# Six front projections in two rounded passes instead of one fp32 pass, with GpSimd preparing the weights, on one Trainium2 core

## The reference, cut to what matters

```python
def _fp8_linear_pertensor(x, wq, w_scale, in_scale):
    xq = _div_clamp_fp8(x, in_scale)          # divide, clip, round to fp8
    return jnp.einsum('bsi,oi->bso', xq * in_scale, wq) * w_scale
...
ln_out = _ln(hidden_states, ln_w, ln_b)
q = _ln(_fp8_linear_pertensor(ln_out, wq, ...), qln_w, qln_b)
k = _ln(_fp8_linear_pertensor(ln_out, wk, ...), kln_w, kln_b)
v = _fp8_linear_pertensor(ln_out, wv, ...)
core = _gqa(q, k, v)
qx = _ln(_fp8_linear_pertensor(ln_out, wqx, ...), qxln_w, qxln_b)
kx, vx = jnp.split(cond @ w_kv_x.T, 2, axis=-1)
xout = _gqa(qx, _ln(kx, kxln_w, kxln_b), vx)
catq = _div_clamp_fp8(concat([core, xout]), proj_smooth)
x = x + catq @ wproj.T * (proj_in_scale * proj_w_scale)
...
w = lut[idx]          # last block: three 256 x 688 tables of weights
```

## Time and profile before

| | |
|---|---|
| median of 3 runs | 498.17 us (496.26 to 504.01) |
| the profiled execution | 496.25 us, its span 494.5 us |
| mean granted TensorE clock | 0.979 |
| PE busy | 453.7 us (92%), 2305 matmuls |
| DVE busy | 354.5 us (72%) |
| ACT busy | 250.2 us (51%) |

### The profile page before, as it was taken

How to read it: one execution, slowest core, us unless ns; L and a number is a source line. 1 busy time by engine, 2 the same in 40 slices (tenths; PEclk the granted TensorE clock), 3 DMA queues, 4 the chain that set the end, 5 groups by cost and what they waited for, 6 DMA issues and landing times.

```text
span 494.5 us, 6607 instructions
## 1 busy us (share of the span) xinstructions
PE 453.7 (92%) x2305; PEld 308.7 (62%) x2311; DVE 354.5 (72%) x722; ACT 250.2 (51%) x784; POOL 27.3 (6%) x36
## 2 busy tenths in 40 slices
PE   5969898699899999999999999998987999989987
PEld 2424444477768575767667775856743888636566
DVE  5884859749797869699896889886765665435631
ACT  1476788867663786866767577553011330120120
POOL 0000000004000010100010010100020010000000
PEclk9999999769999999999999999999998999999999
DMA  8263210405100374644648753890058477300000
GB/s 309 95 270 137 85 62 25 170 3 192 44 1 1 107 144 120 135 113 100 154 107 212 233 113 101 175 340 1 1 180 340 160 195 179 112 6 1 1 0 21
DMA packets 14046, 58.69 MB, mean 119 GB/s; under 512 B 1792, under 2 KB 2624, under 8 KB 12480
## 3 DMA queue, kind: packets, MB, share of 16 engines
q1 hardware_dynamic: 10992, 41.80, 23.2%
q0 software_dynamic: 3024, 16.52, 16.9%
HBM read 41.53 MB, written 0.26 MB: 85 GB/s over the span
## 4 chain that ended last, share of the span: by engine, by line
PE 71%; DVE 16%; ACT 9%; issue 2%; DMA 1%; SPq 0%; DVEq 0%; ACTq 0%
PE PS L455 10%; PE PS L428 8%; PE PS L430 7%; PE PS L429 7%; PE PS L1035 6%; PE PS L363 5%; PE PS L1514 3%; PE PS L1046 3%; PE PS L475 3%; ACT raw_dt.float L1617 2%; PE PS L502 2%; PE PS L1145 2%; ACT raw_dt.float L1597 2%; ACT zu_dt.float L1628 2%; PE PS L1481 1%
## 5 line engine op out<-in xcount | busy, mean ns | idle before, releaser
L570 ACT ACTIVATE sq_dt.float<-PS 128x128 bf16<-128x128 f32 x256 | 67.3, 278 | 33.6 <-PE PS L430 27.1
L455 PE MATMUL PS<-s_dt.float,ctx_ring_dt.float 128*128 128x512 f32 x128 | 57.7, 593 | 2.0 <-DVE px_dt.float L787 2.0
L428 PE MATMUL PS<-wkc_dt.float32r,ctx_hi_dt.float32r 128*128 128x512 f32 x128 | 54.3, 425 | 0.4
L570 ACT ACTIVATION_READ_ACCUMULATOR sq_dt.float<-PS 128x1 f32 x256 | 53.1, 207 | 0.0
L430 PE MATMUL PS<-wkc_dt.float32r,ctxT_ring_dt.float32r 128*128 128x512 f32 x128 | 50.8, 397 | 0.0
L429 PE MATMUL PS<-wkT_dt.float32r,ctx_hi_dt.float32r 128*128 128x512 f32 x128 | 50.7, 396 | 0.0
L1481 PE MATMUL PS<-wch_dt.float,xs_dt.float 128*128 128x512 f32 x96 | 42.1, 593 | 0.0
L363 PE MATMUL PS<-consts_dt.float 128*128 128x512 bf16 x141 | 34.3, 401 | 6.3 <-DMA consts_dt.float<-in_consts 5.5
L455 PEld LDWEIGHTS PS<-s_dt.float,ctx_ring_dt.float 128*128 128x128 f32 x128 | 23.6, 190 | 25.7 <-issue 23.0
L641 ACT ACTIVATE luttmp_dt.float<-low_bit_dt.float,vec_dt.float,small_dt.float 128x1536 f32<-128x1536 uint8 x24 | 38.4, 1653 | 0.0
L648 DVE SCALAR_TENSOR_TENSOR luttmp_dt.float<-idx_dt.float,luttmp_dt.float 128x1536 f32<-128x1536 uint8 x21 | 36.4, 1750 | 0.0
(11 more groups left out here) (276 smaller groups left out, 844.1 us busy)
## 6 DMA issues: line engine op xcount, KB each, us to landing
lutw_dt.float<-luttmp_dt.float POOLq DMA_DIRECT2D x21, 768.0 KB, 6.7
wch_dt.float<-in_chunks SPq DMA_DIRECT2D x6, 1024.0 KB, 4.8
ctxT_ring_dt.float<-in_ctxT SPq DMA_DIRECT2D x8, 512.0 KB, 3.3
ctx_ring_dt.float<-in_ctx SPq DMA_DIRECT2D x8, 512.0 KB, 3.7
keysT_dt.float<-in_ctxT SPq DMA_DIRECT2D x8, 512.0 KB, 7.4
keys_dt.float<-in_ctx SPq DMA_DIRECT2D x8, 512.0 KB, 9.3
luttmp_dt.float<-in_idx SPq DMA_DIRECT2D x3, 768.0 KB, 6.3
zu_dt.float<-in_wproj SPq DMA_DIRECT2D x1, 2048.0 KB, 7.2
```

What stands on the lines that cost most here:

```text
L428: nc.tensor.matmul(o, x_hi, hi[:, c, :], start=c == 0, stop=False)
L455: last = nc.tensor.matmul(bank(5 + c), keysr[k][:, t, c * 128:c * 128 + 128], sS[k][:, t, :], start=t == 0, stop=t == KT - 1)
L570: last = nc.scalar.activation(sq[:, (4 * hf + g) * D:(4 * hf + g + 1) * D], bank(hf)[:, g * D:(g + 1) * D], ACT.Square, accum_out=ssq[:, k ...
```

## The change

- `xs` stays the fp8 value, rounded into fp32r by the last operation of `round_fp8`; `L1719` is gone. GpSimd multiplies each weight chunk by `in_scale` instead (two instructions of 128 x 1024), copies it rounded into `wch_hi` (128 x 2048), and subtracts that to leave `wch_lo` (128 x 2048). `project(n)` makes four banks from `wch_hi` and then adds the `wch_lo` products: 16 fp32r matmuls for 8 fp32 ones.
- GpSimd waits for the chunk's load, and from chunk 2 on for projection n-2.
- `turn(4)` moves from banks 0 to 3 to the rotating banks 4 to 7, behind the first tile of the step-0 keys; PE's order in the transition is rewritten, and ACT reads projection 5 in two halves around `normalise(4)` and takes its squares earlier.
- DVE's step 0 is `first_step`: score tiles before `quantize_core(1)`, no `term`, `low_bits` at the end. `lut_gap` and `pscale` are computed near the start of the front.
- Table step k moves from loop step k to k+1; `term(6)` and `term(7)` lie in the MoE, ACT's `leaf(6)` in step 7.

```diff
             def project(n):
                 pe.wait_ge(xs_ready, SCALED.index(VARIANT[n]) + 1)
-                pe.wait_ge(ld_chunk[n % 2], 16 * (n // 2 + 1))
+                pe.wait_ge(chunk_hi, n + 1)
                 for q in range(4):
                     j, hf = q // 2, q % 2
                     if n:
                         pe.wait_ge(proj_read, 4 * n - 3 + q)
                     for c in range(CT):
+                        nc.tensor.matmul(bank(q), xs[:, VARIANT[n], c, j * 128:j * 128 + 128],
+                                         wch_hi[n % 2][:, c, hf * 512:hf * 512 + 512], start=c == 0, stop=False)
+                pe.wait_ge(chunk_split, n + 1)
+                for q in range(4):
+                    j, hf = q // 2, q % 2
+                    for c in range(CT):
                         last = nc.tensor.matmul(bank(q), xs[:, VARIANT[n], c, j * 128:j * 128 + 128],
-                                                wch[n % 2][:, c, hf * 512:hf * 512 + 512],
-                                                start=c == 0, stop=c == CT - 1)
+                                                wch_lo[n % 2][:, c, hf * 512:hf * 512 + 512],
+                                                start=False, stop=c == CT - 1)
                     last.then_inc(proj_full, 1)
...
+            def split_chunk(n):
+                pool.wait_ge(ld_chunk[n % 2], 16 * (n // 2 + 1))
+                if n > 1:
+                    pool.wait_ge(proj_full, 4 * (n - 1))
+                for c in range(CT):
+                    scaled_w = nc.gpsimd.tensor_scalar(wch[n % 2][:, c, :], wch[n % 2][:, c, :],
+                                                       col("in_scale", VARIANT[n] * CT + c), None, ALU.mult)
+                step(scaled_w)
+                nc.gpsimd.tensor_copy(wch_hi[n % 2], wch[n % 2]).then_inc(chunk_hi, 1)
+                pool.wait_ge(chunk_hi, n + 1)
+                nc.gpsimd.tensor_tensor(wch_lo[n % 2], wch[n % 2], wch_hi[n % 2], ALU.subtract).then_inc(chunk_split, 1)
+            pool.wait_ge(ld_const, 32)
+            for n in range(NCH):
+                split_chunk(n)
...
             def scaled_input(n):
-                step(round_fp8(step, CT * T, xs[:, n].rearrange("p c t -> p (c t)")))
-                for c in range(CT):
-                    last = nc.vector.tensor_scalar(xs[:, n, c, :], xs[:, n, c, :], col("in_scale", n * CT + c), None,
-                                                   ALU.mult)
-                last.then_inc(xs_ready, 1)
+                round_fp8(step, CT * T, xs_wide[:, n * CT * T:(n + 1) * CT * T], xs[:, n].rearrange("p c t -> p (c t)"))\
+                    .then_inc(xs_ready, 1)
...
-            mix_core(3)
-            scores_core(4)
             pe.wait_ge(wk_split, 1)
+            pe.wait_ge(proj_read, 22)
             keys(0, 0, range(1))
+            turn(4)
+            keys(0, 0, range(1, 2))
+            mix_core(3)
+            scores_core(4)
+            keys(0, 0, range(2, KT))
             mix_core(4)
-            keys(0, 0, range(1, KT))
             scores(0, 0)
-            project_core((0, 1))
+            project_core((0,))
             maxima(0)
+            project_core((1,))
             spread(0)
             keys(1, 1)
             project_core((2, 3))
...
+            def first_step():
+                quantize_core(0)
+                key_scale(0, 0)
+                score_tiles(0, 0)
+                quantize_core(1)
+                lo_of_context(dve, 1, 1)
+                turn_beta()
+                maxima(0)
+                shift(0, 0)
+                quantize_core(2)
+                quantize_core(3)
+                lo_of_A(dve, 1)
+                lo_of_context(dve, 2, 0)
+                for m in range(3):
+                    low_bits(m)
+                key_scale(1, 1)
...
             for e in range(2, NE):
                 activate(e, e % 2)
                 add_expert(e - 1, (e - 1) % 2)
-                if e <= 4:
-                    term(dve, LUTN // 2 - 1, e - 2)
+                term(dve, LUT_STEPS + (e - 2) // 3, (e - 2) % 3)
```

More of the change, by code:

```diff
@@ L133, in build @@
         tensors = {(name, fp32): tensor(name, fp32) for name in size}
-        for name in ("wkc", "wkT", "ctx_hi0", "ctx_hi1", "ctxT_ring", "A_hi", "A", "catx", "A_first", "beta"):
+        for name in ("wkc", "wkT", "ctx_hi0", "ctx_hi1", "ctxT_ring", "A_hi", "A", "catx", "A_first", "wpx_hi", "xs", "wch",
+                     "wch_hi0", "wch_hi1"):
             tensors[name, fp32r] = tensor(name, fp32r)
@@ L296, in build, with round_fp8 @@
         t_q = buf("qtmp", 512, skip=768)
-        def round_fp8(step, n, dst):
+        def round_fp8(step, n, dst, out=None):
             step(nc.vector.tensor_scalar(m_bf[:, 0:n].bitcast(u16), y_bf[:, 0:n].bitcast(u16), 0x7F80, None,
@@ L304, in round_fp8 @@
             step(nc.vector.tensor_tensor(dst, y_bf[:, 0:n], m_bf[:, 0:n], ALU.add))
-            return nc.vector.tensor_tensor(dst, dst, m_bf[:, 0:n], ALU.subtract)
+            return nc.vector.tensor_tensor(dst if out is None else out, dst, m_bf[:, 0:n], ALU.subtract)
         wkn = buf("raw", G * C, skip=2048)
@@ L714, in step @@
                     lo_of_context(dve, b + 2, k)
-                if table:
-                    term(dve, b, 1)
+                term(dve, b - 1, 1)
                 if pair is not None:
@@ L719, in step @@
                     quantize_values(pair, 1)
-                if table:
-                    term(dve, b, 2)
+                term(dve, b - 1, 2)
                 if late_pair is not None:
@@ L812, in loop_dve @@
             nc.vector.memset(nt[:, 29:30], 0.0).then_inc(v_read, 1)
-            table = vec[:, COL["lut"]].rearrange("p (k two) -> p k two", two=2)
-            self_step(nc.vector.tensor_tensor(lut_gap, table[:, :, 1], table[:, :, 0], ALU.subtract))
-            self_step(nc.vector.tensor_tensor(pscale, col("proj_w_scale"), col("proj_in_scale"), ALU.mult))
-            lo_of_context(dve, 1, 1)
-            low_bits(0)
-            low_bits(1)
-            key_scale(0, 0)
-            step(0, 0)
+            first_step()
             dve.wait_ge(bits_ready, 3)
@@ L1490, in turn @@
                 for i in range(4):
-                    if n == 4:
-                        pe.wait_ge(proj_read, 20 + i + 1)
-                        o = bank(i, 2, T)
-                    else:
-                        o = bank(ring(f"turn{n}", i), 2, T)
+                    o = bank(ring(f"turn{n}", i), 2, T)
                     for k in range(4):
@@ L1500, in turn @@
                                                    raw[RAW_SLOT[n]][:, j, c0:c0 + 128], ident)
-                    last.then_inc(low_full if n == 4 else ring_full, 1)
+                    last.then_inc(ring_full, 1)
             def cross_queries(n):
@@ L1699, in _ @@
             step(nc.vector.reciprocal(inv_smooth, vec[:, COL["smooth"]]))
+            table = vec[:, COL["lut"]].rearrange("p (k two) -> p k two", two=2)
+            step(nc.vector.tensor_tensor(lut_gap, table[:, :, 1], table[:, :, 0], ALU.subtract))
+            step(nc.vector.tensor_tensor(pscale, col("proj_w_scale"), col("proj_in_scale"), ALU.mult))
             nc.vector.tensor_copy(bk, col("kxln_b").broadcast_to([128, 32])).then_inc(bk_ready, 1)
@@ L1791, in core_scores @@
                 if low:
-                    dve.wait_ge(low_full, 5)
-                    nc.vector.transpose(at_s[low].rearrange("p a q -> p (a q)"), bank(3)).then_inc(low_read["dve"], 1)
-                    dve.wait_ge(low_read["dve"], 1)
+                    dve.wait_ge(low_full, 1)
+                    nc.vector.transpose(at_s[low].rearrange("p a q -> p (a q)"), bank(3)).then_inc(low_read, 1)
+                    dve.wait_ge(low_read, 1)
                 else:
```

105 lines of the change are left out of this document (49 added, 56 removed).

## The result

The kernel after takes 529.59 us (median of 4 runs, 527.38 to 532.25), against 497.22 us before in the same series (4 runs): 1.065 times, 95% interval 1.062 to 1.069. The profiled execution took 527.38 us, its span 525.6 us.

What follows compares the result with a forecast made beforehand. The front was taken as a chain through DVE and ACT, with DVE's small operations held by GpSimd. 13 + 17.4 + 4.1 + 3.0 - 1.8 - 11.4 + 3 + 0.9 = +28.2 on 496.25: 525 us, range 490 to 540.

Steps and rivals of the forecast that it cites:

- Rival 1: Front: GpSimd doesn't hold up DVE, so the front gains and the kernel takes 482 us; chance 0.16.
- Rival 2: Front: unequal turns, only the first of a run of DVE instructions waits; 505 us, give or take 8; chance 0.12.
- Rival 3: PE stays at 1.2 GHz through the front, fp32 cross-query matmuls taking twice 7.8 us; 538 us; chance 0.04.
- A: Front until projection 0's statistics: DVE's held instructions alternate with GpSimd's on chunks 0 and 1, making xs late; +13 us.
- B: Front, chunks 2 and 3: 29 held DVE instructions before the cross-query matmuls, eight waiting a GpSimd instruction each; +17.4 us.
- C: Front, chunk 4: DVE's second L1770 wait for GpSimd's scalings and copy; +4.1 us.
- D: Front, chunk 5: subtraction falls partly on statistics, the rest holds the small chain; +3.0 us, range 0 to 4.5.
- Weights' own wait: Front: PE's wait for split weights costs nothing behind A, as both passes are ready before xs.
- Faster projections: Front: the faster later projections gain nothing, being covered by ACT and DVE.
- Transition: Between front and loop: turn(4) no longer waits for ACT, keys fill PE's holes, score tiles come earlier; -11.4 us.
- Clock: Front: PE idles before projection 0 and turn(0), then runs at a lower clock; +3 us, from none to 7.
- tail and table: End of the kernel: the moved table term before the last add_expert is newly exposed; +0.9 us.

Runs made afterwards that it cites:

- e4: e3 plus GpSimd's scalings, copy and subtraction for six chunks on its own memory, results unused: 528.19 us.
- e9: Kernel after with GpSimd's copy cut into four pieces and its subtraction into eight, same values: 518.73 us, 1.044 of before.
- e1: Kernel after with the constant 0.05 instead of the in_scale column in GpSimd's scalings: 529.25 us profiled; others 520.13, 530.58 and 529.01.
- e7: Kernel after with a second operation, add 0.0, in GpSimd's scalings, same values: 529.88 us.
- e2: Kernel after with GpSimd only copying each chunk, no scaling or subtraction, both passes reading the rounded copy: 497.81 us, 1.000 of before.
- e3: Kernel after with the old front (one fp32 pass, multiplication on DVE, no GpSimd work there), new transition, table and tail kept: 494.7 us, 0.995 of before.
- e8: e3 with the three casts of the table's indices on ACT instead of GpSimd: 489.26 us, 0.985 of before; second series 488.47 us, 0.983.

## Why the prediction was right, point by point

**The mechanism** held: GpSimd and DVE take turns, instruction by instruction, and this sets the time. e4 shows it without any wait for weights. Rival 1 (no hold) is out. Rival 2 (unequal turns) is out as well: L1770 and e9 show one turn each, and the loss is 32 us and not 9. Rival 3 (PE at 1.2 GHz through the whole front) is out: PEclk is 0.5 to 0.6 in three of the nine slices of the front and 0.7 to 0.9 in the others, and the cross-query matmuls take 9.8 and 7.1 us, not twice 7.8.

**Sum.** Predicted +28.2 on the profiled execution, measured +31.1 (525.6 less 494.5). The terms were less good than the sum, and that their errors offset each other is luck:

- *A, +13:* measured +4.3. Two things were mis-sized. One is the scaling: the 1.04 us of the earlier trace rows are those of L1229, which has two operations, and the scalings have one. They take 2.9 us each, and I had a scaling hold DVE for its whole duration, where it holds 1.05. The other is the load: chunk 0 came to GpSimd at 10.51 in this execution and not at 8.9. So the subtraction began at 18.39, when `scaled_input(0)` was through, and `xs` was ready at 16.2 and not at 29. How much is due to the load, two other traces with the same slow form show: with the chunk at 8.10 (e4) and at 8.88 (e1) the subtraction fell on `scaled_input(0)`, and A is 11.7 and 7.1. e7 gave the form that I had counted with, with the chunk at 8.56, and there A is +11.6 (36.59), GpSimd's front work is 52 us and its busy time 78.4, near my 13, 52 and 80.
- *B, +17.4:* the first cross-query matmuls come 23.2 us later, so B, with L1719's share in it, is 18.9. But A and B aren't separate terms: after, e4 and e1, with A at 4.3, 11.7 and 7.1, have these matmuls at 60.88, 60.02 and 59.75. Together I had 30.4, and 23.2 was measured. I forecast "near 65" (my own terms add up to 66 to 68) and read 60.88 (63.10 in e7). L1719 is also taken off once too often in my sum: the seven instructions in A leave it out already.
- *C, +4.1:* the second ones are 25.0 late, +1.8 more, and L1769 at 89.41 takes 3.24 for 0.19 beside chunk 4's subtraction: 4.9 together.
- *D, +3.0:* L1772 (1.77) and L1775 (4.38) beside chunk 5 cost 5.8, and nothing hid them. Mis-sized, outside the 0 to 4.5 that I gave.
- *Weights' own wait, nothing behind A:* PE waits 2.44 and 0.88 us for them, and up to 5.83 ahead of projection 1, but e4, without those waits, is as slow. They lie beside DVE's.
- *Faster projections, nothing:* e2 agrees, with the copies' holds still in it.
- *Transition, -11.4:* measured -6.4 in after and -4.0 in e3. The term that failed is "I leave 2.3 to DVE": I had these index casts in front of me in the earlier trace rows, had used them as evidence for the hold, and didn't ask what they would fall on once moved. They fell on the rounding that PE waits for. Without them (e8) it is -9.4; the 2.0 that are left stay open.
- *Clock, +3, and tail and table, +0.9:* the front's sum, 33.1, is 4.3 + 18.9 + 4.9 + 5.8 = 33.9 less what overlaps, clock included: the cross-query matmuls take 9.78 us for 7.8. The tail lost 4.3 us. In e3, with the same instructions, it loses nothing (nor in e7, and 0.4 in e4), so the table's move is free and the 4.3 is clock: after ran the state-space block's output matmuls (402 to 407) at 0.50 and the readout's 64 matmuls in 5.31 us for 3.66. Why the clock fell there in some executions and not in others stays open.

The error of -8.7 in A was offset by +5.0 in the transition, +3.4 in the tail and +2.8 in D: the sum was nearer than its parts.

**Chances.** The forecast's case came true, and its price lies in the range. The edits of the change outside the front are worth having: 0.5% as they stand (e3), 1.5 to 1.7% with the index casts off GpSimd (e8).

## What to carry to other kernels

Work given to GpSimd isn't free because GpSimd is idle: it is paid for by DVE, one turn per instruction, and the price is the hold of GpSimd's instruction (3.9 us of a 4.6 us subtraction, 1.05 of a 2.9 us scaling) times the turns that DVE needs while GpSimd is at work. In these traces the statistics and the reductions weren't held (the sixteen statistics of a chunk take 3.19 us beside a subtraction in e1 and 3.18 at rest; L1753 takes its own 2.29 beside a copy). Put such work where DVE idles or waits for PE, or on an idle ACT, or, if it must lie beside DVE, cut it into short instructions. To see whether a helper engine hurts, run its instructions on memory of their own in the old kernel; that one run (e4) told the hold from the wait for weights, which no view of the trace could.

## What the runs showed that I had not expected

- On GpSimd, 128 x 1024 with one operation takes 2.78 to 2.9 us and with two operations 1.03 to 1.15 us, for constants and for a column alike. The slow form held DVE for only 1.05 us of it, so making it fast gained nothing here.
- A subtraction of GpSimd's of 128 x 2048 cost DVE 3.9 us on average, a DVE instruction of 0.17 us taking up to 4.4 us.
- 36 us more of DVE's busy time became 33.5 us of the kernel's: in this front nearly no held instruction was off the path.
- PE idle for 4 us ahead of sixteen matmuls cost 2.8 us more by the clock (6.38 for 3.61 us), and with the wait at 1.67 us nothing. In after the wait was 4.03 and the sixteen took 5.17.
